# xDeepFM on one core: x0's rows and the dense layers' inputs read back by DMA from rounded halves that are dumped once a tile

## The reference, cut to what matters

```python
emb = tables[feat_idx, sparse]                    # [B, 26, 32]
linear_out = lin_sparse_w[feat_idx, sparse].sum(-1) + dense @ lin_dense_w
x0 = xk = emb
for w, bb in ((conv1_w, conv1_b), (conv2_w, conv2_b)):
    hp = einsum('bhd,bmd->bhmd', xk, x0)          # all products of two fields, for each of 32 d
    xn = sigmoid(einsum('oi,bid->bod', w, hp) + bb)   # 128 outputs
    xk, kept = xn[:, :64], xn[:, 64:]
    res.append(kept)
cin_out = concat(res).sum(-1) @ cin_w + cin_b     # the sums over d
h1 = tanh(concat(emb, dense) @ W1 + b1)           # 845 -> 1024 -> 512 -> 256
h2 = tanh(h1 @ W2 + b2); h3 = tanh(h2 @ W3 + b3)
out = linear_out + cin_out + h3 @ deep_w + deep_b + bias
```

## Time and profile before

| what | value |
| --- | --- |
| median of 3 runs | 1645.41 us |
| profiled execution, its own time | 1642.12 us |
| its span | 1640.3 us |
| granted TensorE clock, mean | 0.995 |
| TensorE (PE) busy | 1566.3 us, 95% |
| VectorE (DVE), ScalarE (ACT), GpSimd (POOL) busy | 1143.2, 704.7, 763.8 us |
| DMA queue of SyncE, packet time as a share of 16 engines' span | 66.0% |

### The profile page before, as it was taken

How to read it: one execution, slowest core, us unless ns; L and a number is a source line. 1 busy time by engine, 2 the same in 40 slices (tenths; PEclk the granted TensorE clock), 3 DMA queues, 4 the chain that set the end, 5 groups by cost and what they waited for, 6 DMA issues and landing times.

```text
span 1640.3 us, 23407 instructions
## 1 busy us (share of the span) xinstructions
PE 1566.3 (95%) x6840; PEld 681.2 (42%) x6840; DVE 1143.2 (70%) x992; ACT 704.7 (43%) x981; POOL 763.8 (47%) x631
## 2 busy tenths in 40 slices
PE   0599999999999999999999999999999997999998
PEld 0233333333333333333333333333333336787876
DVE  3287878787878787878787878787878783434432
ACT  1344444343444444444344444343444424444543
POOL 7657474757474656565655655664742010000000
PEclk9999999999999999999999999999999999999999
DMA  4688787888887888888888888888888762232231
GB/s 93 124 195 199 189 198 192 194 193 191 196 194 194 194 194 190 193 188 193 195 194 194 194 191 192 193 195 193 196 194 193 185 150 92 92 101 86 89 107 39
DMA packets 111803, 277.60 MB, mean 169 GB/s; under 512 B 26036, under 2 KB 46804, under 8 KB 111704
## 3 DMA queue, kind: packets, MB, share of 16 engines
q1 hardware_dynamic: 98456, 270.11, 66.0%
q0 software_dynamic: 13312, 7.06, 5.3%
HBM read 270.03 MB, written 7.04 MB: 169 GB/s over the span
## 4 chain that ended last, share of the span: by engine, by line
PE 94%; POOL 2%; DVE 1%; ACT 1%; issue 1%; DMA 0%; ACTq 0%; DVEq 0%; POOLq 0%
PE y L636 45%; PE xn L630 21%; PE bc L750 16%; PE bc L616 5%; PE bc L623 3%; PE bc L599 2%; POOL emb L443 2%; PE bc L608 1%; DVE xb L554 0%; ACT sq L806 0%; DVE hp L554 0%; DVE x_lo L563 0%; PE xn L767 0%; DMA sum<-sparse 0%; DMA emb<-table,idx_stage 0%
## 5 line engine op out<-in xcount | busy, mean ns | idle before, releaser
L554 DVE TENSOR_TENSOR hp<-bc,xk 128x1024 f32<-128x1024 f32 x384 | 448.9, 1219 | 264.2 <-PE bc L616 264.2
L554 DVE TENSOR_TENSOR xb<-xb,xk 128x1024 f32<-128x1024 f32 x448 | 581.4, 1355 | 22.8 <-ACT xk L811 22.8
L443 POOL DMA_INDIRECT emb<-table,idx_stage x416 | 495.8, 1192 | 145.9 <-issue 130.5
L636 PE MATMUL y<-xb,w2s 128*64 128x512 f32 x1792 | 423.6, 599 | 0.3 <-ACT r L816 0.3
L636 PE MATMUL y<-hp,w2s 128*64 128x512 f32 x1536 | 368.2, 600 | 0.0
L630 PE MATMUL xn<-sq,w1s 128*128 128x512 f32 x768 | 363.0, 609 | 5.4 <-ACT sq L806 3.2
L806 ACT ACTIVATE sq<-bc 128x1024 f32<-128x1024 f32 x192 | 182.9, 1027 | 261.3 <-PE bc L623 261.3
L810 ACT ACTIVATE xk<-xn,bias 64x512 f32<-64x512 f32 x128 | 87.3, 682 | 376.4 <-PE xn L630 376.4
L458 POOL TENSOR_TENSOR r<-r 128x512 f32<-128x512 f32 x96 | 148.7, 1549 | 144.1 <-ACT r L816 98.4
L630 PEld LDWEIGHTS xn<-sq,w1s 128*128 128x128 f32 x768 | 136.6, 191 | 183.3 <-issue 157.1
L636 PEld LDWEIGHTS y<-xb,w2s 128*64 128x64 f32 x1792 | 117.2, 136 | 214.6 <-issue 188.3
(11 more groups left out here) (63 smaller groups left out, 1056.4 us busy)
## 6 DMA issues: line engine op xcount, KB each, us to landing
xb<-x_rows SPq DMA_DIRECT2D x896, 256.0 KB, 4.9
w_raw<-W SPq DMA_DIRECT2D x32, 448.0 KB, 3.3
w_raw<-W SPq DMA_DIRECT2D x16, 512.0 KB, 3.3
emb<-table,idx_stage POOLq DMA_INDIRECT x416
x_rows<-deep_t SPq DMA_DIRECT2D x16, 384.0 KB
w_raw<-W SPq DMA_DIRECT2D x8, 256.0 KB, 2.7
hp<-select SPq DMA_DIRECT2D x2, 512.0 KB, 4.8
x_rows<-deep_t SPq DMA_DIRECT2D x16, 45.0 KB
```

What stands on the lines that cost most here:

```text
L443: nc.gpsimd.indirect_dma_start(out=emb[:, m, :], out_offset=None, in_=table, in_offset=bass.IndirectOffsetOnAxis(ap=idx_stage[:, m:m + 1], ...
L554: nc.vector.tensor_tensor(product(n)[:, :], x[:, :], xk[sl % 2][:, :], ALU.mult).then_inc(multiplied, 1)
L636: last = nc.tensor.matmul(y2[H * c:H * c + H, :], w2s[:, ORDER[n], :], src[:, c * CHUNK:(c + 1) * CHUNK], start=(n == 0), stop=(n == PAIRS ...
```

## The change

1. `turn_x0`, `make_high`, `make_low` and `halves` go. In step 1 of a tile `emb` is turned in three parts D0 (3 transposes), D1 (2) and D2 (2); of each part ScalarE makes a plain copy in `deep_t`, now one tile large, and a rounded copy in `deep_halves`; VectorE subtracts (`lower_deep`), SyncE dumps `deep_t` (`dump`) and, in its work for step 2, both halves (`dump_halves`) to DRAM, and reads `x0t` back from there, four DMAs a step (`load_rows`).
2. The order of a step becomes K | contract 8 to 12 of the last | D in step 1 | spread 3, 4 | first 0 | contract 0, 1, 2 | spread 6, 7 | first 1 | spread 9, 10 | contract 3 to 7. The T fills go, so a tile has 39 fills (42 before), over the same three slots.
3. Of a pair of fields the second one lies on partitions 32 to 95, the first one on 0 to 31 and 96 to 127, so `spread_by_dma` issues three DMAs a product (64, 32 and 32 partitions).
4. `x_hi` and `x_lo` of a group are read by 16 DMAs (`load_x`) from the dumped halves, the first group's while the last tile runs; `upper_x` and `lower_x` go. These tiles, `w_raw` and the first `w_hi` and `w_lo` have space of their own, and the first weights are split ahead of the CIN stage.
5. r1 and r2 are summed in a fifth slice (`total`), so ScalarE waits for fewer of GpSimd's sums.
6. Three of the end's terms (dense, linear, sum of r1) move into the last step of the CIN stage; the bias is added by one instruction over 97 partitions.

```diff
-ORDER = [3, 10, 4, 0, 7, 11, 5, 1, 8, 2, 9, 12, 6]
-BY_PE = (3, 4, 7, 8, 9, 10)
+ORDER = [0, 1, 2, 3, 8, 4, 5, 9, 6, 7, 10, 11, 12]
+BY_PE = (3, 4, 6, 7, 9, 10)
 STEP_WORK = (
     ("fill", (("K", 0), ("K", 1), ("K", 2))),
-    ("of_last", (9, 10, 11, 12)),
-    ("fill", (("T", 0), ("D", 0), ("D", 1))),
+    ("of_last", (8, 9, 10, 11, 12)),
+    ("fill", (("D", 0), ("D", 1), ("D", 2))),
+    ("fill", (3, 4)),
     ("first", 0),
-    ("fill", (3, 4)),
     ("of_this", (0, 1, 2)),
+    ("fill", (6, 7)),
     ("first", 1),
-    ("fill", (7, 8)),
-    ("of_this", (3, 4)),
     ("fill", (9, 10)),
-    ("of_this", (5, 6, 7, 8)),
+    ("of_this", (3, 4, 5, 6, 7)),
 )
-SL_DEEP = 2
-DEEP_PARTS = range(0, 4), range(4, KD)
+SL_DEEP = 1
+DEEP_PARTS = range(0, 3), range(3, 5), range(5, KD)
...
+PAIR_ROWS = ((1, slice(QUARTER, 3 * QUARTER)), (0, slice(0, QUARTER)), (0, slice(3 * QUARTER, P)))
...
+            def dump_halves(t):
+                sp.wait_ge(deep_lowered, t * 2 + 2)
+                hold()
+                for i in range(2):
+                    sp.dma_start(x0_halves[bass.ds(t, 1), i, 0:(KD - 1) * P, :].rearrange("t (k p) b -> p (t k) b", p=P),
+                                 deep_halves[:, i, 0:KD - 1, :].bitcast(F32)).then_inc(halves_dumped, 16)
+                    sp.dma_start(x0_halves[bass.ds(t, 1), i, (KD - 1) * P:M * ROW, :].rearrange("t p b -> p (t b)"),
+                                 deep_halves[0:LAST_E, i, KD - 1, :].bitcast(F32)).then_inc(halves_dumped, 16)
...
+            def load_rows(t, sl):
+                for half in range(2):
+                    rows = x0_halves[bass.ds(t, 1), half, :, :].rearrange("t (m e) b -> (t m) e b", e=ROW)
+                    for c in range(2):
+                        first = sl * STEP_D + c * Q
+                        start = H * c + half
+                        sp.dma_start(x0t[sl][start:start + 2 * M:2, :].bitcast(F32),
+                                     rows[:, first:first + Q, :].rearrange("m d b -> m (d b)")).then_inc(x0_loaded[sl % 2], 16)
...
             def spread_by_dma(t, sl, i):
-                for f in range(2):
+                for f, parts in PAIR_ROWS:
...
+                        if i == 2 and sl == SL_DEEP + 1 and ahead > 0:
+                            dump_halves(t + 1)
+                        if i == 3 and sl == SL_DEEP + 1 and ahead > 0:
+                            await_halves(t + 1)
+                        if i == 3 and (sl < 2 or ahead > 0):
+                            if is_first and sl == 0:
+                                sp.wait_ge(filled, PRO_FILLS)
+                            load_rows(t + (sl + 2) // STEPS, (sl + 2) % STEPS)
+                    if sl == SL_DEEP and ahead > 0:
+                        dump(t + 1)
+                    if sl == 2 and ahead == 0:
+                        sp.wait_ge(dense_dumped, 64)
+                        load_x(0, 0, 1)
...
+            sp.wait_ge(w1_step, 7)
+            dump_halves(0)
             dump(0)
+            sp.wait_ge(pads_cleared, STEPS)
+            await_halves(0)
+            for sl in range(2):
+                load_rows(0, sl)
             await_dump(0)
...
+                        if n == 7 and sl == SL_DEEP and ahead > 0:
+                            dve.wait_ge(halves_dumped, t * (32 * DUMPS) + 32 * DUMPS)
+                            lower_deep(t + 1)
...
+                            if final:
+                                ...
+                                add_term(cwd[:, :], dense_rows, start=True)
+                                add_linear()
...
                     if final:
+                        pe.wait_ge(r1_step, TILES * SUMS)
+                        add_term(cw1[:, :], sum1)
                         for n in LEFT:
                             pe.wait_ge(multiplied, multiplied_by(s, n))
                             contract(n)
...
+            def turned_deep(slot, t, part, is_first=False):
+                ...
+                for rows, k, k_end, at in pieces:
+                    src = bc[slot][rows, at:at + (k_end - k) * P].rearrange("p (k b) -> p k b", b=P)
+                    last = nc.scalar.activation(deep_t[rows, k:k_end, :], src, ACT.Copy)
+                last.then_inc(deep_copied, 1)
+                for rows, k, k_end, at in pieces:
+                    src = bc[slot][rows, at:at + (k_end - k) * P].rearrange("p (k b) -> p k b", b=P)
+                    last = nc.scalar.activation(deep_halves[rows, 0, k:k_end, :], src, ACT.Copy)
+                last.then_inc(deep_rounded, 1)
...
-            for g in range(GROUPS):
-                r = slice(32 * g, 32 * g + 1)
-                nc.scalar.activation(orow[r, :], xn[r, 0:CHUNK], ACT.Identity, bias=bias_out[r, :]).then_inc(row_ready, 1)
+            rows = slice(0, 32 * (GROUPS - 1) + 1)
+            nc.scalar.activation(orow[rows, :], xn[rows, :], ACT.Identity, bias=bias_out[rows, :]).then_inc(row_ready, 1)
```

More of the change, by code:

```diff
@@ L79, in step_fills @@
         fills = [use for use in fills if not is_k(use)]
-    if ahead == 0 and sl >= STEPS - 2:
-        fills = [use for use in fills if not is_t(use)]
     if ahead == 0 or sl != SL_DEEP:
@@ L88, in is_k @@
     return isinstance(use, tuple) and use[0] == "K"
-def is_t(use):
-    return isinstance(use, tuple) and use[0] == "T"
 def is_d(use):
@@ L159, in build @@
         idf = sb("idf", [P, P])
-        w_raw = [sb("w_raw0", [P, F1N // P, P])]
+        w_raw = [sb(f"w_raw{i}", [P, F1N // P, P]) for i in range(2)]
         bd1 = sb("bd1", [P, F1N // P])
@@ L324, in over_groups @@
             group(GROUPS - 1, False, True)
-        X_AFTER = {F1N // P + i: range(2 * i, min(2 * i + 2, KD)) for i in range(-(-KD // 2))}
         def x_tile(k):
@@ new lines, in load_x @@
+            def load_x(g, part, parts):
+                loads = []
+                for i, x in enumerate((x_hi, x_lo)):
+                    for k in range(KD):
+                        rows = P if k < KD - 1 else LAST_E
+                        src = x0_halves[bass.ds(g * (CHUNK // P), CHUNK // P), i, k * P:k * P + rows, :]
+                        loads.append((x[0:rows, k, :].bitcast(F32).rearrange("p (t b) -> p t b", b=P),
+                                      src.rearrange("t p b -> p t b")))
+                    loads.append((x[LAST_E:LAST_K, KD - 1, :].bitcast(F32), dense_halves[i, :, bass.ds(g * CHUNK, CHUNK)]))
+                for dst, src in loads[part * X_LOADS // parts:(part + 1) * X_LOADS // parts]:
+                    sp.dma_start(dst, src).then_inc(x_loaded, 16)
@@ L393, in tile @@
                     s = t * STEPS + sl
-                    if sl == SL_DEEP + 1 and ahead > 0:
-                        dump(t + 1)
                     for i, n in enumerate(BY_DMA):
@@ L467, in _ @@
             gather(range(M))
-            make_low(0)
             def free_emb(t, dense_turned):
@@ L586, in deep_group @@
                         nc.vector.tensor_tensor(h_lo[:, a, :], h_raw[a % 2][:, :], h_hi[:, a, :], ALU.subtract).then_inc(h_low, 1)
-                    if a in X_AFTER and not is_last:
-                        for k in X_AFTER[a]:
-                            lower_x(g + 1, k)
             over_groups(dve, deep_group)
@@ L594, in _ @@
         def _(pe):
-            def turn_x0(slot, sl):
-                for q in range(Q):
-                    d = sl * STEP_D + 2 * q
-                    last = nc.tensor.matmul(bc[slot][:, q * P:(q + 1) * P],
-                                            halves[:, d:d + 2, :, :, :].rearrange("p c g i m -> p (c g i m)"),
-                                            idr[:, :], start=True, stop=True)
-                last.then_inc(filled, 1)
             def turn_deep(slot, ks):
-                rows = emb[:, 0:M, :].rearrange("p m e -> p (m e)")
+                rows = emb[:, :, :].rearrange("p m e -> p (m e)")
                 for at, k in enumerate(ks):
@@ new lines, in _ @@
+            upper_w(0, 0)
+            def turned_deep(slot, t, part, is_first=False):
+                ks = DEEP_PARTS[part]
+                whole = len(ks) if ks[-1] < KD - 1 else len(ks) - 1
+                pieces = [(slice(0, P), ks[0], ks[0] + whole, 0)]
+                if whole < len(ks):
+                    pieces.append((slice(0, LAST_E), KD - 1, KD, whole * P))
+                if part == 0 and not is_first:
+                    act.wait_ge(dumped, t * (16 * DUMPS))
+                    act.wait_ge(halves_dumped, t * (32 * DUMPS))
+                for rows, k, k_end, at in pieces:
[6 more added lines that the diff above has]
+                last.then_inc(deep_rounded, 1)
@@ L908, in deep_group @@
                         nc.scalar.activation(h_hi[:, a, :], h_raw[a % 2][:, :], ACT.Copy).then_inc(h_high, 1)
-                    if a in X_AFTER and not is_last:
-                        for k in X_AFTER[a]:
-                            upper_x(g + 1, k)
             over_groups(act, deep_group)
```

315 lines of the change are left out of this document (151 added, 164 removed).

## The result

The changed kernel takes 1686.62 us (median of 4 runs, 1683.47 to 1690.13) beside 1645.58 us for the kernel before: ratio 1.0252, 95% interval 1.023 to 1.0274. In a second set on the same kind of machine it was 1687.51 beside 1644.11, ratio 1.0271 (1.0254 to 1.0288). Forecast were 1621 us and a faster kernel. All ratios leave out executions in a slower state of the machine, among them one of 3187 us in the first experiment, so where some were left out a median of all runs stands off its ratio. The profiled execution has a span of 1688.3 us, 48.0 above the one of before.

The account below looks back on a forecast made before the run. The prediction took TensorE to set the pace of both stages; its terms, savings less the pause after D and costs at start and last step, summed to -24.7 us, from 1645.4 to 1621 us, range 1602 to 1648.

Parts of the forecast that it names:

- SyncE's own stream: CIN steps: 25 issues for 14, near 0.5 us each, 12.5 us of a 19.3 us step; cost nothing.
- T fills and fewer groups: TensorE's CIN steps: dropped T fills save 31.0 us, fewer groups of contractions 11.3 us; plain step 19.3 us.
- the new neighbours: CIN step order: spread before first-layer contraction, and that before a product's; no cost taken, -0.1 to +0.18 us a step allowed.
- The pause after D: CIN D step: TensorE waits 1.4 us for ScalarE's copies before spreads 3, 4; 15 tiles, 21.0 us lost.
- DMA: CIN tiles: 17.3 MB in about 78.9 us, 219 GB/s, 96% of saturation; cost 0, at most +6 us a tile.
- the case that the ports matter: CIN tiles: if broadcasts spanning both partition halves use more SBUF ports, DMA share is 0.85 or less, otherwise 0.95.
- Rival A: CIN stage: the DMA queue sets the pace, tile about 82 us, time 1669 us, slower; chance 0.12.
- The start: Before CIN: K fills at 58 us, 5 us later than before, bounds 3 and 8.
- The last step: End of CIN: load_x ahead of the last broadcasts costs +3 us, terms moved in cost +3.1 us.
- Between the stages and tail: CIN to second dense accumulation: 9.0 us saved, about 5.8 left; after the last accumulation: 5.0 us saved.
- The dense stage: Dense stage: 0.5 us saved by dropping upper_x and lower_x; load_x costs 0, at most +2 us a group.

Follow-up runs that it names:

- the first experiment: The changed kernel with two broadcasts of 64 partitions a product instead of three: 1657.44 us, ratio 0.9963 to the kernel before.
- the best version: The changed kernel with ScalarE issuing the steady tiles' x0t reads, "first 0" between D and spreads 3, 4, and the last tile's loads split by step: 1610.62 us, ratio 0.9801.
- "first 0" back: The version with all three edits (reads by ScalarE, "first 0" moved, loads split), but "first 0" put back behind spreads 3, 4: 1687.07 us, ratio 1.0118.
- the base: The changed kernel with reads by ScalarE, "first 0" moved and loads split, rerun beside versions with one part undone: 1630.04 us, ratio 0.9802.

## Why the prediction was wrong

The step that failed is "SyncE's own stream": "25 issues a step for 14, near 0.5 us each: 12.5 us of 19.3 ... Nothing." Three things were missing. First, the row gave the length of one issue (0.55 for a dump; the median of a broadcast in that trace is 0.47), not the distance to the next. That was to be had from the trace of before: of 80.56 us a tile SyncE waited 612.1 / 16 = 38, so 58 issues took 42, 0.73 each, and 106 of them would take 77 of the 79.4 us that I forecast for a tile; measured are 75. That 77 comes so near is in part luck: one price for all is too high for the 84 broadcasts (61 us for the 54 measured) and too low for the 16 reads (12 for 17). Second, the wait for the halves' landing, 2.1: the prediction has it, but as a delay within one step and not as a part of the stream's sum. Third, the turn of the loop, 5.4 us in the tile shown and 4.3 in the mean, where the turns of before took 0.3. A stream as long as the tile never catches up.

The Trainium skill says in "Perfetto Trace Analysis", section "What "DMA-bound" means", that the issuing engine's sequencer is a bound of its own beside the DMA engines; the trace agrees (26% of the chain is SyncE's queue), and I had weighed the engines' share only. The Trainium skill's page "DMA: Bandwidth & Descriptors", section "Issuing engines are not separate DMA queues", calls what a second issuing engine saves usually small; here it was 3.8% of the middle of the kernel.

Where the loss lies: K is first filled 7.8 us later, the CIN stage from there to its end is 49.8 longer (1350.6 for 1300.8), the stretch to the second accumulation 8.9 shorter, the dense stage 3.8 longer, the tail 4.6 shorter: 47.9 of the 48.0. The CIN stage had been forecast at 15.2 shorter. Of the 65.0 missed there, 7.1 are the last step, and the other 57.9 are 3.7 us for each of the 15.75 tiles before it.

The terms beside it:

*T fills and fewer groups: right.* Steps in which SyncE is not late, of the kernel after:

```profile
1347.04 0.51 PE L677 MATMUL bc<-x0t,sel 32*128 32x512 f32 x4
...
1366.40 0.51 PE L677 MATMUL bc<-x0t,sel 32*128 32x512 f32 x4
```

19.36 us, 19.3 forecast; the new neighbours cost nothing. With SyncE's loop written out a tile takes 79.65 us (79.4 forecast), and 78.10 with "first 0" moved (79.4 less the pause of 1.4: 78.0).

*The pause after D: right.* TensorE and ScalarE in the D step:

```profile
768.22 0.51 PE L677 MATMUL bc<-x0t,sel 32*128 32x512 f32 x4 [1.24 <-ACT deep_halves L876]
```

```profile
767.13 0.49 ACT L876 ACTIVATE deep_halves<-bc 128x384 fp32r<-128x384 f32 x1
...
767.76 0.41 ACT L876 ACTIVATE deep_halves<-bc 128x256 fp32r<-128x256 f32 x1
```

1.24 each and 18.7 in 15 times, for 1.4 and 21.0. The rows at 768.22 and 851.61 show the same pause 83.39 us apart, where 79.4 had been foreseen.

*DMA: the size right, the rival wrong.* 17.3 MB a tile were moved, at 207 to 221 GB/s, without the engines binding; the share, 0.78 to 0.85, is the one that the prediction had for the case that the ports matter. Rival A had the right sign through the wrong resource, and its test, VectorE waiting in each tile, cannot tell the two apart; SyncE's own waits can.

*The start: too small.* The first K fill:

```profile
60.91 1.65 PE L684 MATMUL bc<-x0t,sel 64*128 64x512 f32 x6 [13.20 <-DMA x0t<-x_halves]
```

60.91 for 58, within the bound of 8.

*The last step: too small.* It took 31.2 us for 18.0, +13.2 for the +6.1 of `load_x` and the terms together. The 16 loads were counted as bytes in the queue; they cost SyncE's time first, and the waits then cost clock:

```profile
1369.09 5.05 SPq L435 DMA_DIRECT2D x_hi<-x_halves  x7
1374.18 0.83 SPq L435 DMA_DIRECT2D x_hi<-dense_halves  x1
1375.06 5.86 SPq L435 DMA_DIRECT2D x_lo<-x_halves  x7
1380.96 0.60 SPq L435 DMA_DIRECT2D x_lo<-dense_halves  x1
1381.69 12.82 SPq L441 DMA_DIRECT2D xb<-x_rows  x21
```

12.6 us before the last step's broadcasts. TensorE waits 5.3 us in the step (1.3 before), the terms take 2.9, and most of the rest stands beside a granted clock of 0.50 (1.2 GHz) from 1390.9 to 1404.6 us, which came after TensorE had waited 2.38 us for a product: eight matmuls to `y` take 3.92 us there and 1.89 at the full clock. With SyncE's loop written out the step still takes 30.1, and with the loads split as well 23.6.

*Between the stages and tail: right.* The second accumulation starts 5.9 us after the CIN stage's end (5.8 forecast), idle 0.86; from the last accumulation to the end 5.8 us for 10.5, -4.6 (-5.0 forecast). The end, which answers to the earlier trace rows:

```profile
1417.49 0.47 PE L826 MATMUL bc<-x_hi,w_hi 128*128 128x512 f32 x1 [0.86 <-DVE w_lo L617]
```

```profile
1685.36 0.69 ACT L966 ACTIVATE orow<-xn,bias_out 97x512 f32<-97x512 f32 x1 [2.09 <-PE xn L749]
```

*The dense stage: wrong sign.* 265.0 us from the second accumulation for 261.2. In 250 us TensorE makes 1070 matmuls for 1086, at the full clock and equally busy, while the DMA share rises from 0.30 to 0.45; the best version shows it too (1068, 0.44). By the records of single matmuls each one starts 231.2 ns after the last, before 227.4, whatever it multiplies. The higher DMA share does not seem to be the reason: within the kernel after the distance is 231 ns where that share is under 0.2 and where it is over 0.8 alike. What slows them stays open.

## What to carry to other kernels

Count the issuing engine as an engine: issues times the distance from one issue to the next, plus every wait in its stream and the turn of its loop, against the period; the waits that it has today are its room. A late broadcast looks the same for a full DMA queue and for a full issuing stream: the DMA share and the issuing engine's own waits tell them apart. The cures are to move issues to an engine that waits anyway (0.9801 here) or to write the loop out (0.9783), both with "first 0" moved and the last tile's loads split; writing out alone gave 0.9979 for 1.0252.

## What the runs showed of the hardware

- The turn of SyncE's loop is free or costs some microseconds. It took about 0.3 us (0.0 to 0.7) with 236, 292 and 298 recorded instructions a turn, and 2.4 to 4.8 in the mean of a run with 306, 348, 354 and 388 (single turns 1.0 to 5.7). The profile's queue for instructions moves 16 or 17 packets in the kernels without the pause, 77 or 78 in those with it, 62 with two tiles a turn and 29 with the loop written out:

```profile
q14 instruction: 78, 0.64, 0.1%
```

That is five packets of 8192 bytes more a turn, and in the changed kernel one of them moves within each of the 12 pauses (at 821.2 us in the one shown above), so the body is fetched again at each turn. The Trainium skill has the mechanism ("Runtime: NRT & Kernel Launch", section "Instruction fetch mechanics": a taken branch to instructions no longer held fetches them by DMA first); the limit that it gives is 512 instructions, and the records, which may leave some out, pause from between 298 and 306 on. Whether the length alone decides, or also where the body lies, no run tells.
- The time to issue a DMA depends on its shape and on the stream that it stands in. Medians on SyncE: a broadcast to 64 partitions 0.47 us in the kernel before and 0.53 in the changed one, one to 32 partitions 0.42 in the changed kernel and 0.35 with four such a product, a read of 26 rows to every second partition 0.79; the distance to the next is 0.15 to 0.25 more in a loop, where address arithmetic stands between, and 0.04 to 0.07 with the loop written out.
- In four of the seven sets of runs engines stood still, ScalarE for up to 13.2 us, with nothing on the core to end it, and kernels lost more there than in the quiet sets: with "first 0" back 3.2% more than the base, where the pause is worth 18.7 us. The branches of ScalarE's loop have no pause (0.3 us) in these runs. What is behind it stays open.
